# Moving one gather in 32 from GpSimd to SyncE and ScalarE in a two-layer graph kernel

## Chip, core and metric

The kernel runs on one core of one Trainium2 chip. The metric is the device time of one execution in microseconds; lower is better. The core has five engines with a queue each: TensorE (PE, with its weight loads shown as PEld), VectorE (DVE), ScalarE (ACT), GpSimd (POOL) and SyncE (SP), and 16 DMA engines that all queues share. In the rows below a name with a q (SPq, ACTq) is the queue of an engine: register work and the issue of transfers.

## What is computed

Two graph layers on 12500 nodes of 256 features and 200000 edges. The edges come sorted by dst. Each layer sums rows of a node table over the edges that end in a node, multiplies by weights, and normalizes.

```
# layer 0
out_deg = max(segment_sum(ones, src), 1)
t1  = x @ W1
msg = (t1[src] + (x[src] * x[dst]) @ W2) / (sqrt(out_deg[src]) * sqrt(out_deg[dst]))
embed = leaky_relu(where(in_cnt > 0, t1 + segment_sum(msg, dst), 0) + b)
x = layernorm(x + embed / max(norm(embed), 1e-12))
# layer 1
xt  = x @ W.T + b
out = segment_sum(xt[src], dst) / (deg + 1)
x = layernorm(x + out)
```

## The kernel before

The edges are cut into 1563 tiles of 128 edges, and 32 tiles make a round: 49 rounds per layer, the last with 27 tiles. One round also finishes one pair of node blocks (2 x 128 nodes).

GpSimd gathers. For each tile it issues one indirect DMA (L405) that reads 128 table rows of 1 KB, one for each edge, into one of 32 slots of `ring`. The indices stand in `idx`. TensorE multiplies each slot by a 0/1 matrix `dst_hot` (L1004), which adds the rows of a group of 8 tiles by destination into one of four sum buffers. After each of these it loads a register in `pace()` (L993). VectorE makes the 0/1 matrices (L710) and adds each group into `acc`, a view of `big` (L736).

ScalarE releases the slots. After each group k of round i has been multiplied (`groups_done`), `refill` copies the 8 indices of group k of round i+1 into `idx` (L514), and GpSimd waits for that copy only. So a gather of round i+1 may start once its group in round i has been multiplied.

Each round i also finishes the pair of blocks i-1. The steps stand in one fixed order on each engine:

- layer 0, VectorE: `mix` (L746, L748) after group 1. TensorE: transposes in `turn_halves` (L977) after tile 19, products with the weights (L988) after tile 23; these wait for `a_ready`.
- ScalarE, between the refills of groups 1 and 2: `clear_sums` (L521) in layer 0 or `take_sums` (L527) in layer 1, then `take_turned` (L536), two copies out of the banks into `a_t`, each of which sets `a_ready`. After the refill of group 2: `roots` (L542 and L544 in layer 0, L544 alone in layer 1). Then the refill of group 3.
- VectorE, after group 2: `finish_sums` and `moments`, with ScalarE's roots in between; after group 3: `norm`.
- SyncE, in `next_pair`: when `var_ready` comes, two loads of x (L304 in layer 0, L300 in layer 1), and when `out_ready` comes, two stores (L309, L313). It has nothing else to do in the rounds.

The order of work is written out by hand. Each engine runs its own queue in order, and only semaphores tie the engines together.

Of the kernel before, what the change touches and what calls it, by code (L numbers as in the profile page):

```python
# [24 lines left out]
P = 128  # L25
D = 256
KF = D // P
NODES = 12500
# [5 lines left out]
U = 32  # L34
# [35 lines left out]
DUMP = NPAD  # L70


def gnn(nc, x, src, dst, w1, w2, b0, wl, b1, out):
# [6 lines left out]
    with ExitStack() as ctx:  # L80
# [19 lines left out]
        src_hi = sb("src_hi", [P, TILES], BF16)  # L100
        count_to = sb("count_to", [P, P, PAIR], BF16)
# [115 lines left out]
        gather_turn = sem("gather_turn")  # L217
        dst_hot_made = sem("dst_hot_made")
# [42 lines left out]
        def _(sp):  # L261
# [69 lines left out]

            sp.wait_ge(flag_made, 1)
            disordered = sp.value_load(flag[0:1, 0:1], min_val=0, max_val=1)
            with sp.If(disordered == 0):
                for layer in range(2):
                    for s in range(2):
                        load_x(layer, 0, s, s)
                    with sp.Fori(0, ROUNDS - 2) as m:
                        next_pair(layer, m)
                    next_pair(layer, ROUNDS - 2)  # L340
# [28 lines left out]
        def _(g):  # L369
# [58 lines left out]
            with g.If(disordered == 0):  # L428
                for layer in range(2):
                    if layer == 1:  # L430
                        g.wait_ge(table1_whole, 1)
                    if layer == 1:
                        for q in range(4):
                            gather_quarter(layer, 0, q)
# [30 lines left out]
        def _(act):  # L465
# [80 lines left out]
            def round_(layer, i, finish):  # L546
                for q in range(4):
# [13 lines left out]
            with act.If(disordered == 0):  # L561
                for layer in range(2):
                    round_(layer, 0, False)
                    with act.Fori(1, ROUNDS) as i:
                        round_(layer, i, True)
# [333 lines left out]
        def _(pe):  # L899
# [95 lines left out]
            def round_(layer, i, finish, end=U):  # L995

                for k in range(GR):
# [3 lines left out]
                    for u in tiles:  # L1001
                        rounds_before = layer * (ROUNDS if u < FINAL else ROUNDS - 1) + i
                        pe.wait_ge(rows_in[u], 16 * (rounds_before + 1))
# [15 lines left out]
            with pe.If(disordered == 0):  # L1019
                for layer in range(2):  # L1020
                    round_(layer, 0, False)
                    with pe.Fori(1, ROUNDS - 1) as i:
                        round_(layer, i, True)
# [42 lines left out]
```

## Time and profile before

| what | value |
|---|---|
| median of 3 runs | 4180.89 us (4180.33 to 4181.39) |
| profiled execution | 4172.7 us, its span 4170.9 us |
| POOL busy | 3033.6 us, 73% |
| PE busy | 3387.3 us, 81% |
| DVE busy | 1603.1 us, 38% |
| ACT busy | 460.4 us, 11% |
| mean granted TensorE clock | 0.719 |
| DMA | 237098 packets, 489.88 MB, mean 117 GB/s |

Busy time leaves out the issue of transfers, register work and waits. A small share of busy time on ACT or SP therefore does not say how long its queue stands at a wait. The layers' rounds fill the span from about 240 to 4157 us; before them lies the preparation of the edges and of the scaled table, without gathers of the rounds.

### The profile page before, as it was taken

The page shows a single profiled execution, that of the slowest core. Times are in us where ns is not written, and L with a number is a line of the kernel's source. Part 1 is how long each engine was busy: PE and PEld are TensorE (multiplying, and loading weights), DVE is VectorE, ACT ScalarE, POOL GpSimd, SP SyncE. Part 2 cuts the span into 40 slices and gives each one's busy share as a digit, 9 for nine tenths or more (in the row PEclk, how much of TensorE's full clock was granted, in tenths as well). Part 3 has the DMA queues.
Part 4 walks back from the last instruction along what each step waited for, and adds up shares of the span by engine and source line. Part 5 has one row for each costly group of instructions (what it writes and reads, how often), then busy time and mean ns, then how long its engine had stood idle before and what let it go on. Part 6 is the DMA issues. An engine that isn't in the chain of part 4 may idle for free.

```text
span 4170.9 us, 49033 instructions
## 1 busy us (share of the span) xinstructions
PE 3387.3 (81%) x9623; PEld 1749.8 (42%) x9623; DVE 1603.1 (38%) x3315; ACT 460.4 (11%) x1457; POOL 3033.6 (73%) x3179
## 2 busy tenths in 40 slices
PE   6568888888888888888878887888888888888887
PEld 5434444444444444444443343334333343343433
DVE  9954334343343433434342323333233332333333
ACT  8910000000000000000000000000000000000000
POOL 5167777777777777777757777777777777777776
PEclk8777767777677776777776767767677667777666
DMA  6244444343443434444333444444443444434443
GB/s 189 68 138 119 114 120 119 114 119 114 119 119 114 119 114 120 119 115 120 115 94 111 119 115 119 114 120 117 118 119 114 120 117 117 120 114 119 117 117 106
DMA packets 237098, 489.88 MB, mean 117 GB/s; under 512 B 57665, under 2 KB 137044, under 8 KB 237076
## 3 DMA queue, kind: packets, MB, share of 16 engines
q0 software_dynamic: 151072, 409.95, 34.7%
q1 hardware_dynamic: 86004, 79.66, 5.9%
q8 instruction: 11, 0.18, 0.0%
q14 instruction: 11, 0.09, 0.0%
HBM read 450.84 MB, written 38.54 MB: 117 GB/s over the span
## 4 chain that ended last, share of the span: by engine, by line
POOL 68%; issue 25%; DVE 4%; PE 1%; DVEq 1%; POOLq 1%; DMA 0%; SPq 0%; ACT 0%; ACTq 0%
POOL ring L405 68%; DVE hot_space L600 2%; DVEq L592 0%; PE banks L1004 0%; DVE big L663 0%; PE banks L988 0%; POOLq L435 0%; POOLq L402 0%; PE banks L916 0%; DVE big L724 0%; POOLq L403 0%; DVEq L635 0%; DMA ring<-in_dst 0%; SPq L270 0%; DMA ring<-x,idx 0%
## 5 line engine op out<-in xcount | busy, mean ns | idle before, releaser
L1004 PE MATMUL banks<-ring,hot_space 128*128 128x257 f32 x6252 | 2901.9, 575 | 671.6 <-DMA ring<-x,idx 326.5
L1004 PEld LDWEIGHTS banks<-ring,hot_space 128*128 128x128 f32 x6252 | 1315.7, 256 | 2192.9 <-DMA ring<-x,idx 1045.3
L405 POOL DMA_INDIRECT ring<-x,idx x1563 | 1486.5, 951 | 505.7 <-issue 475.9
L405 POOL DMA_INDIRECT ring<-scaled_x,idx x1531 | 1455.9, 951 | 476.4 <-issue 465.6
L736 DVE SCALAR_TENSOR_TENSOR big<-banks,here_mask,big 128x257 f32 x784 | 343.7, 480 | 2086.7 <-PE banks L1004 2086.6
L710 DVE TENSOR_TENSOR hot_space<-banks,dst_rel 128x1024 f32<-128x1024 f32 x395 | 483.7, 1224 | 198.1 <-issue 197.6
L514 ACT COPY idx<-src_col 128x8 int32 (+1 forms) x392 | 77.3, 197 | 2528.2 <-PE banks L1004 2528.2
L988 PE MATMUL banks<-w_s,a_t 128*128 128x256 f32 x784 | 184.2, 389 | 0.0
L482 ACT ACTIVATE dst_rel<-columns,halves 128x128 bf16<-128x128 f32 x576 | 161.3, 374 | 4.5 <-DVE halves L629 4.5
L988 PEld LDWEIGHTS banks<-w_s,a_t 128*128 128x128 f32 x784 | 146.5, 192 | 34.6 <-issue 16.0
L977 PE MATMUL banks<-ident,halves 128*128 128x128 f32 x588 | 131.2, 388 | 13.2 <-DVE halves L748 8.7
L977 PEld LDWEIGHTS banks<-ident,halves 128*128 128x128 f32 x588 | 112.8, 207 | 46.6 <-issue 23.0
L916 PE MATMUL banks<-hot_space 128*128 128x98 bf16 x1280 | 91.1, 236 | 40.0 <-DVE hot_space L600 39.2
L536 ACT COPY a_t<-banks 128x512 f32<-128x512 f32 (+1 forms) x196 | 90.4, 479 | 282.6 <-PE banks L977 282.2
L413 POOL DMA_INDIRECT r_edge<-r_table,idx x32 | 32.0, 999 | 112.1 <-DMA r_table<-e 102.7
L988 PE MATMUL banks<-wt_s,a_t 128*128 128x256 f32 x392 | 106.1, 418 | 1.4
L916 PEld LDWEIGHTS banks<-hot_space 128*128 128x128 bf16 x1280 | 77.5, 113 | 51.7 <-DVE hot_space L600 44.8
L600 DVE TENSOR_TENSOR hot_space<-src_lo,count_to 128x2048 bf16<-128x2048 bf16 x80 | 97.6, 1221 | 0.2
L760 DVE SCALAR_TENSOR_TENSOR e<-banks,scal,b_s 128x256 f32<-128x256 f32 x98 | 42.9, 479 | 134.2 <-PE banks L988 134.2
L988 PEld LDWEIGHTS banks<-wt_s,a_t 128*128 128x128 f32 x392 | 76.8, 206 | 30.6 <-issue 20.2
L815 DVE TENSOR_SCALAR out_t<-out_t,mv,scal 128x256 f32<-128x256 f32 x196 | 75.7, 428 | 7.7
L600 DVE TENSOR_TENSOR hot_space<-src_hi,count_to 128x1568 bf16<-128x1568 bf16 x80 | 77.6, 969 | 0.0
(112 smaller groups left out, 773.5 us busy)
## 6 DMA issues: line engine op xcount, KB each, us to landing
ring<-x,idx POOLq DMA_INDIRECT x1563, 2.8
ring<-scaled_x,idx POOLq DMA_INDIRECT x1531, 2.8
x<-out_t SPq DMA_DIRECT2D x98, 128.0 KB, 2.6
x_t<-x SPq DMA_DIRECT2D x98, 128.0 KB, 2.3
big<-in_x SPq DMA_DIRECT2D x1, 12416.0 KB
x_t<-in_x SPq DMA_DIRECT2D x97, 128.0 KB, 2.2
result<-out_t SPq DMA_DIRECT2D x97, 128.0 KB, 1.9
scaled_x<-big SPq DMA_DIRECT2D x6, 1792.0 KB, 13.8
```

Of the source, the lines that this page charges most:

```text
L405: g.indirect_dma_start(ring[:, u, 0:D], None, table[layer], bass.IndirectOffsetOnAxis(ap=idx[:, u:u + 1], axis=0)).then_inc(rows_in[u], 16)
L482: last = nc.scalar.activation(steps[:, third, t, first:first + size], columns[:, 0:size], ACT.Sign, bias=step_digits[:, digit, bass.ds(n * ...
L514: nc.scalar.copy(idx[:, q * QT:(q + 1) * QT], src_col[:, bass.ds(i * U + U + q * QT, QT)]).then_inc(idx_ready, 1)
L536: nc.scalar.copy(a_t[s][:, 0:parts, :, :].rearrange("p h k n -> p (h k n)"), turned[s][:, 0:parts * D]).then_inc(a_ready[s], 1)
L600: last = nc.vector.tensor_tensor(hots[half], vals.unsqueeze(2).to_broadcast(shape), count_to[:, 0:size, :].unsqueeze(1).to_broadcast(shape ...
L710: last = nc.vector.tensor_tensor(dst_hot[:, buf, :, :], lane_row.unsqueeze(1).to_broadcast([P, GT, P]), rel, ALU.is_equal)
L736: last = nc.vector.scalar_tensor_tensor(here, group_sum(k), here_mask[:, n, bass.ds(i * GR + k, 1)], here, ALU.mult, ALU.add)
L815: nc.vector.tensor_scalar(out_t[s][:, :], out_t[s][:, :], mv[:, s, 0:1], scal[:, 6 + s:7 + s], ALU.subtract, ALU.mult).then_inc(out_ready[ ...
L916: last = nc.tensor.matmul(hist, lo_hot[half][:, t // PAIR, :, t % PAIR], hi_hot[half][:, t // PAIR, :, t % PAIR], start=first and t == 0, ...
L977: last = nc.tensor.transpose(turned[s][:, place:place + P], halves[:, s, h, k * P:(k + 1) * P], ident[:, :])
L988: last = nc.tensor.matmul(project[s], left, right, start=n == 0, stop=n == len(parts) - 1)
L1004: last = nc.tensor.matmul(group_sum(k), dst_hot[:, k % HOTS, u - k * GT, :], ring[:, u, 0:DW], start=u == tiles[0], stop=u == tiles[-1])
```

## The change

In rounds 2 to 47 of each layer (46 rounds, 23 pairs) GpSimd leaves out slot 31, the last of the round (`HAND_U`). For the even round of a pair SyncE fetches the 128 rows of that slot, for the odd round ScalarE. Each does it by 128 separate transfers of one row of 1 KB, whose address comes from a register. The indices are read with a DMA into one partition (`hand_idxs`) and from there into registers (`load`). The rows land in a buffer `hands`, and one more DMA copies the buffer into slot 31 of the ring. TensorE waits on that copy (`hand_in_ring`) in place of the gather. Both buffers lie in space that is free by then.

SyncE issues 64 rows after the copy into the ring and 64 after the next `next_pair`. ScalarE issues 26 rows after the refill of group 0, 12 after group 2's refill and the roots, and 26 after the refill of group 3, in every round of the pairs. GpSimd, ScalarE and TensorE now have loops over pairs or peeled rounds.

```diff
+HAND_U = U - 1
+HAND_REGS = 16
+ACT_ROWS = {0: (0, 26), 2: (26, 38), 3: (38, 64)}
+HAND_PAIRS = (ROUNDS - 2) // 2
...
 (SyncE)
+            def gather_by_hand(layer, j, half):
+                if half == 0:
+                    sp.wait_ge(hand_idx_in[0], 16 * (hand_no(layer, j) + 1))
+                    sp.sem_inc(sync_turn, 1)
+                for first in range(half * P // 2, (half + 1) * P // 2, HAND_REGS):
+                    sp.load(hand_regs, hand_idxs[0][0:1, first:first + HAND_REGS])
+                    for k in range(HAND_REGS):
+                        row = sp.snap(hand_regs[k], min_val=0, max_val=NODES - 1)
+                        sp.dma_start(hands[0][first + k:first + k + 1, :],
+                                     table[layer][bass.ds(row, 1), :]).then_inc(hand_rows_in[0], 16)
+            def hand_to_ring(layer, j):
+                sp.wait_ge(hand_rows_in[0], 16 * P * (hand_no(layer, j) + 1))
+                sp.wait_ge(groups_done, group_no(layer, 2 * j + 1, GR - 1) + 1)
+                sp.dma_start(ring[:, HAND_U, 0:D], hands[0][:, :]).then_inc(hand_in_ring[0], 16)
+            def hand_pair(layer, j):
+                next_pair(layer, 2 * j)
+                hand_to_ring(layer, j)
+                sp.wait_ge(hand_in_ring[0], 16 * (hand_no(layer, j) + 1))
+                gather_by_hand(layer, j + 1, 0)
+                next_pair(layer, 2 * j + 1)
+                gather_by_hand(layer, j + 1, 1)
+                load_hand_idx(layer, j + 2)
...
 (GpSimd)
-                    with g.Fori(1, ROUNDS - 1) as i:
+                    for i in range(0 if layer == 1 else 1, 2):
                         for q in range(4):
                             gather_quarter(layer, i, q)
+                    with g.Fori(2, ROUNDS - 1) as i:
+                        for q in range(4):
+                            gather_quarter(layer, i, q, HAND_U)
...
 (ScalarE)
+            def gather_by_act(layer, j, half, q):
+                if half == 0 and q == 0:
+                    act.wait_ge(hand_idx_in[1], 16 * (act_hand_no(layer, j) + 1))
+                    act.sem_inc(act_turn, 1)
+                    act.wait_ge(hand_in_ring[1], 16 * (act_hand_no(layer, j) + 1))
+                    act.sem_inc(act_turn, 1)
+                first, end = (half * P // 2 + n for n in ACT_ROWS[q])
+                act.load(act_regs[0:end - first], hand_idxs[1][0:1, first:end])
+                for k in range(first, end):
+                    row = act.snap(act_regs[k - first], min_val=0, max_val=NODES - 1)
+                    nc.scalar.dma_start(hands[1][k:k + 1, :],
+                                        table[layer][bass.ds(row, 1), :]).then_inc(hand_rows_in[1], 16)
+            def act_hand_to_ring(layer, j):
+                act.wait_ge(hand_rows_in[1], 16 * P * (act_hand_no(layer, j) + 1))
+                act.sem_inc(act_turn, 1)
+                nc.scalar.dma_start(ring[:, HAND_U, 0:D], hands[1][:, :]).then_inc(hand_in_ring[1], 16)
...
                     refill(layer, i, q)
                     if finish and q == LAST_K + 1:
                         roots(layer, i - 1)
+                    if pair_no is not None and q in ACT_ROWS:
+                        gather_by_act(layer, pair_no, half, q)
+                if pair_no is not None and half == 1:
+                    act_hand_to_ring(layer, pair_no)
...
 (TensorE)
+                        if u == HAND_U and by_hand is not None:
+                            pe.wait_ge(hand_in_ring[by_hand], 16 * (layer * HAND_PAIRS + pair_no + 1 + by_hand))
```

The first place is ScalarE in layer 0, at the refill of group 1 (rows L514 before, L579 after) and the copies into `a_t`. Before:

```order
L514 COPY idx<-src_col 128x8
L512 REGISTER_ALU
L514 ISA [waits groups_done]
L514 COPY idx<-src_col 128x8
L519 ISA
L521 ISA [waits mixed]
L521 COPY big<-zeros 128x514
L532 REGISTER_ALU
L536 COPY a_t<-banks 128x512 [waits halves_turned,projected]
```

After, from the last two rows of the burst behind group 0's refill on (L633 and L634 are one row's register work and its transfer):

```order
L633 ISA
L634 DMA src_lo<-scaled_x 1x256
L577 REGISTER_ALU
L579 ISA [waits groups_done]
L579 COPY idx<-src_col 128x8
L584 ISA
L586 ISA [waits mixed]
L586 COPY big<-zeros 128x514
L597 REGISTER_ALU
L601 COPY a_t<-banks 128x512 [waits halves_turned,projected]
```

The refill of group 1, the clearing and the copies into `a_t` now stand behind 26 transfers and one register load that were not there.

The second place is SyncE in layer 0, at the end of `next_pair`. Before:

```order
L309 ISA [waits out_ready0]
L309 DMA x<-out_t 128x256
L309 ISA [waits out_ready1]
L309 DMA x<-out_t 128x256
L338 REGISTER_ALU
L338 COMPARE_AND_BRANCH
```

After (L370 is the copy into the ring, L360 the load of 16 registers, L363 a row):

```order
L319 ISA [waits out_ready1]
L319 DMA x<-out_t 128x256
L368 ISA
L369 ISA [waits hand_rows_in0]
L370 DMA ring<-src_lo 128x256 [waits groups_done]
L376 REGISTER_ALU
L357 ISA [waits hand_in_ring0]
L360 TENSOR_LOAD src_hi [waits hand_idx_in0]
L362 ISA
L363 DMA src_lo<-scaled_x 1x256
```

Behind the stores SyncE now has waits for its rows, for the last group of the round and for the copy into the ring, and then 64 rows before the next pair's loads.

## Rows read from the trace of the kernel before

**Rows 1.** Page: the chain that ended last by engine, and TensorE's costliest group.
```profile
POOL 68%; issue 25%; DVE 4%; PE 1%; DVEq 1%; POOLq 1%; DMA 0%; SPq 0%; ACT 0%; ACTq 0%
...
L1004 PE MATMUL banks<-ring,hot_space 128*128 128x257 f32 x6252 | 2901.9, 575 | 671.6 <-DMA ring<-x,idx 326.5
```

**Rows 2.** Line L405, layer 0: ns min/median/max, first and last start.
```profile
L405 POOL DMA_INDIRECT ring<-scaled_x,idx x1531: 942/946/1227, 238.8 to 2159.7; - x192
```

**Rows 3.** Timeline of GpSimd in a round of layer 0: start, us, instruction.
```profile
1034.97 0.95 POOL L405 DMA_INDIRECT ring<-scaled_x,idx  x1 [0.30 <-issue]
```

**Rows 4.** Timeline of ScalarE, one round of layer 0.
```profile
1015.33 0.20 ACT L514 COPY idx<-src_col 128x8 int32 x1 [10.51 <-PE banks L1004]
...
1028.51 0.62 ACT L521 COPY big<-zeros 128x514 f32 x1 [3.02 <-DVE halves L748]
1030.99 0.58 ACT L536 COPY a_t<-banks 128x512 f32<-128x512 f32 x1 [1.86 <-PE banks L977]
...
1034.91 0.20 ACT L514 COPY idx<-src_col 128x8 int32 x1 [2.50 <-PE banks L1004]
...
1043.90 0.30 ACT L544 ACTIVATE scal<-mv,epsilon 128x2 f32<-128x2 f32 x1 [2.62 <-DVEq L592]
1044.92 0.20 ACT L514 COPY idx<-src_col 128x8 int32 x1 [0.72 <-PE banks L1004]
```

**Rows 5.** Timeline of TensorE, same round: the products.
```profile
1034.65 3.72 PE L988 MATMUL banks<-w_s,a_t 128*128 128x256 f32 x16
```

**Rows 6.** Timeline of ScalarE, one round of layer 1.
```profile
3018.14 0.62 ACT L527 COPY halves<-big 128x512 f32 x1 [0.87 <-DVE big L736]
3022.53 0.65 ACT L536 COPY a_t<-banks 128x256 f32<-128x256 f32 x2 [3.77 <-PE banks L977]
...
3031.66 0.29 ACT L544 ACTIVATE scal<-mv,epsilon 128x2 f32<-128x2 f32 x1 [4.93 <-DVEq L592]
```

**Rows 7.** Timeline with weight loads, same round: transposes and products.
```profile
3021.32 0.18 PEld L977 LDWEIGHTS banks<-ident,halves 128*128 128x128 f32 x1
...
3026.37 1.99 PE L988 MATMUL banks<-wt_s,a_t 128*128 128x256 f32 x8
```

**Rows 8.** Line L288, a transfer into one partition: ns min/median/max.
```profile
L288 SPq DMA_DIRECT2D base_row<-group_bases x1: 236/236/236, 183.3 to 183.3; - x1
```

**Rows 9.** DMA from 183.2 to 185.2 us, that transfer alone: packets, MB, share.
```profile
q1 hardware_dynamic: 2, 0.00, 0.1%
```

**Rows 10.** Line L304, transfers with an address from a register.
```profile
L304 SPq DMA_DIRECT2D x_t<-in_x x97: 342/355/1628, 220.6 to 2168.6; - x97
L304 SPq FUSED_REGOPS  x94: 55/65/81, 280.4 to 2128.9; - x94
L304 SPq MOVE x_t<-in_x x94: 29/29/29, 280.5 to 2129.0; - x94
```

**Rows 11.** Timeline of SyncE, one round of layer 0.
```profile
1003.83 0.91 SPq L304 DMA_DIRECT2D x_t<-in_x  x2
1006.75 0.91 SPq L309 DMA_DIRECT2D x<-out_t  x2
```

**Rows 12.** Line L993, a load of one register.
```profile
L993 PEldq TENSOR_LOAD <-block_row x3126: 296/302/758, 231.0 to 4155.0; - x196
```

**Rows 13.** Windows of 10 us: PE, PEld, DVE, ACT, POOL busy, PEclk, DMA share, GB/s.
```profile
1014.00:1024.00 10.00, 9.50 (x17) 4.03 (x17) 2.10 (x3) 0.20 (x1) 7.57 (x9) 0.50 0.36 105
...
1034.00:1044.00 10.00, 8.19 (x32) 5.67 (x32) 5.51 (x18) 0.49 (x3) 7.56 (x9) 1.00 0.36 105
```

**Rows 14.** Line L988, layer 0: ns min/median/max.
```profile
L988 PE MATMUL banks<-w_s,a_t x784: 378/379/797, 271.2 to 2180.4; 128*128 128x256 f32 x196
```

**Rows 15.** DMA from 1000 to 1080.4 us: queues, and the loads' landing.
```profile
q0 software_dynamic: 3072, 8.39, 36.3%
q1 hardware_dynamic: 1152, 1.05, 3.8%
...
x_t<-in_x SPq DMA_DIRECT2D x4, 128.0 KB, 2.1
```

More of the change, by code:

```diff
@@ L100, in gnn @@
         src_hi = sb("src_hi", [P, TILES], BF16)
+        hands = [src_lo[:, 2 * n * D:2 * (n + 1) * D].bitcast(F32) for n in range(2)]
+        hand_idxs = [src_hi[0:1, 2 * n * P:2 * (n + 1) * P].bitcast(I32) for n in range(2)]
         count_to = sb("count_to", [P, P, PAIR], BF16)
@@ L217, in gnn @@
         gather_turn = sem("gather_turn")
+        hand_idx_in = [sem(f"hand_idx_in{n}") for n in range(2)]
+        hand_rows_in = [sem(f"hand_rows_in{n}") for n in range(2)]
+        sync_turn = sem("sync_turn")
+        hand_in_ring = [sem(f"hand_in_ring{n}") for n in range(2)]
         dst_hot_made = sem("dst_hot_made")
@@ L334, in _ @@
             with sp.If(disordered == 0):
+                for c in range(len(X_CHUNKS)):
+                    sp.wait_ge(table_stored[c], 16)
                 for layer in range(2):
@@ L544, in roots, with act_hand_no, load_act_idx, round_ @@
                 nc.scalar.activation(pair[3], mv[:, :, 1], ACT.Sqrt, bias=epsilon[:, 0:1]).then_inc(var_rooted, 1)
-            def round_(layer, i, finish):
+            act_regs = [act.alloc_register(f"act_row{k}") for k in range(26)]
+            def act_hand_no(layer, j):
+                return layer * HAND_PAIRS + j
+            def load_act_idx(layer, j):
+                nc.scalar.dma_start(hand_idxs[1][:, :],
+                                    src[bass.ds((2 * j + 3) * U * P + HAND_U * P, P)].rearrange("(a n) -> a n", a=1)
+                                    ).then_inc(hand_idx_in[1], 16)
+            def gather_by_act(layer, j, half, q):
[14 more added lines that the diff above has]
+                nc.scalar.dma_start(ring[:, HAND_U, 0:D], hands[1][:, :]).then_inc(hand_in_ring[1], 16)
+            def round_(layer, i, finish, pair_no=None, half=0):
+                if pair_no is not None and half == 0:
+                    load_act_idx(layer, pair_no)
                 for q in range(4):
@@ L561, in _ @@
             with act.If(disordered == 0):
+                act.sem_inc(hand_in_ring[1], 16)
+                for c in range(len(X_CHUNKS)):
+                    act.wait_ge(table_stored[c], 16)
                 for layer in range(2):
+                    if layer == 1:
+                        act.wait_ge(table1_whole, 1)
                     round_(layer, 0, False)
-                    with act.Fori(1, ROUNDS) as i:
-                        round_(layer, i, True)
+                    with act.Fori(0, HAND_PAIRS) as j:
+                        round_(layer, 2 * j + 1, True, j, 0)
+                        round_(layer, 2 * j + 2, True, j, 1)
+                    round_(layer, ROUNDS - 2, True)
+                    round_(layer, ROUNDS - 1, True)
                     if layer == 0:
@@ L993, in pace, with round_ @@
                 pe.value_load(block_row[0:1, 0:1], min_val=0, max_val=NW - 1)
-            def round_(layer, i, finish, end=U):
+            def round_(layer, i, finish, end=U, by_hand=None, pair_no=0):
                 for k in range(GR):
@@ L1021, in _ @@
                     round_(layer, 0, False)
-                    with pe.Fori(1, ROUNDS - 1) as i:
-                        round_(layer, i, True)
+                    round_(layer, 1, True)
+                    with pe.Fori(0, HAND_PAIRS) as j:
+                        round_(layer, 2 * j + 2, True, by_hand=0, pair_no=j)
+                        round_(layer, 2 * j + 3, True, by_hand=1, pair_no=j)
                     round_(layer, ROUNDS - 1, True, FINAL)
```

34 lines of the change are left out of this document (27 added, 7 removed).

## The prediction

> **What bounds the kernel now.** I read the chain of waits first. It should show GpSimd with the issue gaps between its instructions holding nearly all of the span, and TensorE with idle time that a DMA ended [rows 1]: the gathers set the pace and TensorE waits for them. Next the timeline of GpSimd: a gather of 0.95 us follows the last after 0.30 us of issue, so one costs 1.25 us and no semaphore stands between [rows 3]. From the first and last start of layer 0, 1920.9 us over 1530 steps is 1.2555 us, and 32 of them make a round of 40.18 us [rows 2]. Last I read ScalarE's timeline, because the new work goes there. It looks idle, but three of its stops in a round are waits in a fixed order: on a group, on the transposes before the copies into a_t, and on VectorE for the roots [rows 4, 6].
>
> **What goes.** GpSimd leaves out one gather in 46 rounds of each layer, 92 in all. 92 x 1.25 = 115.0 us [rows 3], and the round becomes 38.93 us if GpSimd still sets it. The profiled execution is 4172.7 us, so that alone gives 4057.7; the median of the runs stands 8.2 above it, which makes 4065.9. What comes next behind GpSimd decides the rest.
>
> **What one row costs the queue that issues it.** No transfer of one row from a register address is in the trace. A transfer into one partition holds SyncE's queue for 0.236 us [rows 8]. Two transfers with register addresses take 0.91 us from the start of one to the end of the other, and each is 0.355, so 0.20 us lies between them: the fused register work of 0.065, a move of 0.029 and gaps [rows 10, 11]. A row thus costs 0.236 + 0.20 = 0.436 us, and I take that on both queues. The low bound is 0.29, the issue and about 0.05 of gap, if the register work is hidden. The high bound is 0.555, the whole step of a 128-row transfer. A register load is 0.30 [rows 12] and with its gap 0.35; I take this for each load of 12 to 26 registers. The far bound is 0.30 for every register, 64 x 0.30 = 19 us a round; I stay with the one instruction, since it is one.
>
> **SyncE.** For a pair of rounds it has 128 x 0.436 = 55.8, eight loads 2.8, eight large transfers in four steps of 0.91, 3.6, its ring copy 0.36 with about 2.1 of landing [rows 10, 15], and some 0.5 for the indices and the branch: 65.2. It also stands 2.0 us twice between the loads of x and the stores [rows 11]: 69 of 77.9 us. It fits, with 9 us left. Behind its waits stand the loads of x for the next mix and the stores, and both have more than ten microseconds until VectorE asks. I cost SyncE at nothing; it would set the pace from a row of 0.50 us on.
>
> **ScalarE.** Here I add up the circle that its queue must close in each round, if it comes late and TensorE waits for it.
> Layer 0, from the first copy into a_t: the copy 0.58, about 0.15 to TensorE, then from the start of the products at 1034.65 to the end of the second root at 1044.20, 9.55 [rows 4, 5]. That is 10.3 us in which ScalarE can issue no row, because the roots stand ahead of the 12 rows. Then the three remaining refills, 0.20 of copy and 0.1 of register work each, 0.9; three register loads, 1.05; the clearing of the sums 0.62 with gaps, 0.8; at the pair's end the landing of the last row 2.1, the copy's issue 0.36 and the next index load about 0.3, per round 1.4. Sum 14.4 us without rows. The 64 rows are 27.9. Together 42.3 us, against 38.93 for the gathers and 40.18 now.
> Layer 1, from take_sums: 0.62, 0.1, the transposes until the copies start 1.2 (3021.32 to 3022.53), one copy 0.33, 0.15, and from the start of the products at 3026.37 to the end of the root at 3031.95, 5.6 [rows 6, 7]: 8.0. With 0.9, 1.05, 1.4 and 0.1 it is 11.4, with the rows 39.3 us.
> In between the two sits a smaller term. The products ran where the granted clock was 1.00 (2.4 GHz), just after TensorE had worked through its stretch at 0.50 (1.2 GHz) [rows 13]. A TensorE that is kept waiting for a_t may run them at the lower level, where one matmul takes 797 ns and not 379 [rows 14]. For the whole set that is at most 3.7 us in layer 0 and 2.0 in layer 1 (their own length again); the least is nothing. I take a fifth, 0.7 and 0.4.
> The rounds then are 43.0 and 39.7 us.
>
> **The sum.** 46 x (43.0 - 40.18) = +130, 46 x (39.7 - 40.18) = -22, together +108 us: 4280.7 in the profiled execution's terms, with the 8.2 us 4289. The 115 us that GpSimd gives back are not to be added; they are the difference to a bound that then no longer holds. The tail, the fetch of the first rows in each layer and the waits for the table (stored long before) I cost at nothing: the first hand slot is wanted at the end of round 2, some 110 us after the layer begins, and 128 rows take 56.
> TensorE itself is no term. Its 671.6 us of waits on DMA [rows 1] are 6.9 us a round, and it gives 1.25 of them away. A late ring copy has a round's slack.
>
> **The rivals.**
> The first is that rows are cheap. In terms of the row price c, layer 0 needs 14.4 + 64c and layer 1 11.4 + 64c. Both fit under 38.93 from c = 0.38 down, and then the whole 115 us come: 4066. With the clock term the kernel is even with before at about c = 0.41. At c = 0.29 ScalarE has 6 us to spare. For it: two register operations might overlap the transfer before; the distance to my 0.436 is small. Against it: on SyncE they visibly did not overlap [rows 11].
> The second is that the two queues hinder each other when both issue. SyncE issues in 56 of some 84 us; if one's 0.236 us had to wait for the other's, a row would grow by 0.03 to 0.05 on average, and to 0.47 where they alternate. At 0.47, layer 0 is 45.2 and layer 1 41.9 with the clock term: 46 x (5.0 + 1.7) = +308, or 4489. If every row cost 0.555, it would be 50.6 and 47.3, +807 or 4988, with SyncE the bound as well (128 x 0.555 + 13.4 = 84.4 per pair). Nothing in the trace speaks to it, since ScalarE issues no transfer in it.
> The Trainium skill, in Perfetto Trace Analysis, section DMA Instruction — HWDGE (DVE, Sync), says that such transfers use one descriptor generator that two sequencers share, and that it is locked for exclusive use. By that rule this rival would hold and the time be near 4489; no run so far shows it.
> The third is that all rows go through one DMA engine. The transfer into one partition left two packets, one of data and one to signal, so it ran on a single engine [rows 9]. All 16 engines were busy 40.1% [rows 15], 31 us of a pair. The hardware queue's mean packet cost is 3.8% x 16 x 80.4 / 1152 = 42 ns; 256 rows with two packets each add 22 us if they all meet on one engine: 53 of 78 us, which is no bound. It decides only from 0.18 us a row on. If a row had to land (about 2.1 us [rows 15]) before that queue's next row moved, a pair would take 128 x 2.1 = 269 us, and the kernel over 12,000.
> On this the Trainium skill, in DMA: Bandwidth & Descriptors, section Why a DMA increments its semaphore by 16 and not by 1, says that a transfer that uses fewer than 16 engines takes the lowest-numbered ones. By that rule all 256 rows of a pair do meet on the first engine; the two packets above agree with one engine, and which one they do not show.
>
> **How the numbers follow.** ScalarE's circle sets the round, with c between 0.41 and 0.46: 0.44, time 4289, its own range 4190 to 4440. Rows cheap enough for a gain: 0.30, times 4066 to 4172. The queues hinder each other: 0.18, 4440 to 4990. One engine or a SyncE bound far above: 0.04. A result within 0.2% of before, which is about what a measurement can tell from no change, is the narrow passage between the first two: 0.04. So faster 0.30, same 0.04, slower 0.66. The range runs from 4062, the whole gain, to 4520, which leaves out the harder half of the second rival and the one engine.
>
> **What would show it.** In the changed profile the steps between rows on ScalarE should be about 0.44 us. The copies into a_t should come right behind the burst and the refill of group 1, TensorE should wait for them before the products in layer 0, and the refills of groups 0 and 1 should come late after their groups. A round should take about 43 us in layer 0 and under 40.2 in layer 1; the layers should differ. GpSimd should then wait for the refill in each round of layer 0, where it now waits for nothing. SyncE should reach its wait for var_ready before it comes. I am wrong if ScalarE still stands waiting for groups 0 and 1 in both layers: then the rounds are 38.9 us and the gain is whole. Steps above 0.5 us, or longer issues where both queues are at work, speak for the second rival; gathers that land much later than before for the third.

## The result, and the profile after

The changed kernel takes 5175.7 us, the median of 4 runs (5172.2 to 5176.3), against 4180.9 for four runs of the kernel before beside it (4180.3 to 4181.4). The ratio is 1.238, 95% interval 1.236 to 1.240: slower, as forecast, but by 995 us and not by 108, and outside the range of 4062 to 4520. The experiments ran in four groups, each on a chip of its own beside the kernel before: in two groups that took about 4171 us, in two 5031 to 5040, and there the two queues' register steps, 44 ns otherwise, took up to 1.5 us (the disturbed chips below). Ratios are taken only within a group.

The page after: the chain that ended last by engine and by line, then three of the costliest groups, with what they waited for in the last column.

```profile
ACTq 53%; issue 18%; PE 10%; DVE 8%; DVEq 4%; DMA 3%; ACT 3%; POOL 2%; SPq 0%; POOLq 0%
ACTq L634 29%; ACTq L631 18%; PE banks L1099 6%; ACTq L633 5%; PE banks L1120 4%; DVEq L703 3%; DVE hot_space L711 2%; POOL ring L470 2%; DMA src_hi<-in_src 1%; PE banks L1088 1%; DVE stats L914 1%; ACT idx L579 1%; DMA src_lo<-x 1%; DMA src_lo<-scaled_x 1%; ACT halves L592 1%
...
L470 POOL DMA_INDIRECT ring<-scaled_x,idx x1485 | 1420.9, 957 | 1074.4 <-ACT idx L579 636.7
...
L1099 PE MATMUL banks<-w_s,a_t 128*128 128x256 f32 x784 | 291.6, 552 | 1245.9 <-ACT a_t L601 1245.9
L1088 PE MATMUL banks<-ident,halves 128*128 128x128 f32 x588 | 120.4, 342 | 1256.1 <-ACT halves L592 1221.7
```

GpSimd held 68% of the chain before [rows 1] and holds 2% now; ScalarE's queue holds 53%: 29% in the issue of its rows (L634) and 18% in its register loads (L631). TensorE, which had waited for a DMA, now waits some 27 us in each of the 46 rounds for a copy that ScalarE makes: `a_t` (L601) in layer 0, `halves` (L592) in layer 1. GpSimd waits for the refills. That is the mechanism that the forecast named, ScalarE's circle, at another size.

ScalarE's timeline over one pair of rounds of layer 0, which answers to [rows 4]: start, length, instruction, count in a burst, and in brackets the idle time before. The stretch from 1506.67 to 1612.52 is one pair.

```profile
1506.67 0.20 ACT L579 COPY idx<-src_col 128x8 int32 x1 [7.54 <-issue]
1512.55 10.16 ACTq L634 DMA_DIRECT2D src_lo<-scaled_x  x26
1523.90 0.50 ACTq L641 DMA_DIRECT2D ring<-src_lo  x1
1527.43 0.23 ACTq L619 DMA_DIRECT2D src_hi<-in_src  x1
...
1531.37 10.20 ACTq L634 DMA_DIRECT2D src_lo<-scaled_x  x26
1541.84 0.20 ACT L579 COPY idx<-src_col 128x8 int32 x1 [13.68 <-issue]
...
1542.63 1.07 ACT L601 COPY a_t<-banks 128x512 f32<-128x512 f32 x2
...
1554.37 0.29 ACT L609 ACTIVATE scal<-mv,epsilon 128x2 f32<-128x2 f32 x1 [2.62 <-DVEq L703]
1557.31 4.65 ACTq L634 DMA_DIRECT2D src_lo<-scaled_x  x12
1562.22 0.20 ACT L579 COPY idx<-src_col 128x8 int32 x1 [7.56 <-PE banks L1120]
1568.10 10.16 ACTq L634 DMA_DIRECT2D src_lo<-scaled_x  x26
...
1612.52 0.20 ACT L579 COPY idx<-src_col 128x8 int32 x1 [7.52 <-issue]
```

The copies into `a_t` stand right behind a burst and a refill, as expected. What was not expected is the time between a refill and the burst that follows it: 5.9 us ahead of the bursts at 1512.55 and 1568.10, 3.4 ahead of 1531.37. Behind the last root it is 2.9, ahead of 1557.31. In it the queue loads index registers. Line L631, ScalarE's register loads, in three short stretches (at 1506.7: 26 words from word 102 of the tile, 38 into its second half; at 1529.1: 26 words from word 0; at 1554.4: 12 words from word 26), and for the whole run, then a row's own instructions and SyncE's loads of 16 words (ns min/median/max, first and last start):

```profile
L631 ACTq TENSOR_LOAD <-src_hi x1: 5702/5702/5702, 1506.7 to 1506.7; - x1
L631 ACTq TENSOR_LOAD <-src_hi x1: 2129/2129/2129, 1529.1 to 1529.1; - x1
L631 ACTq TENSOR_LOAD <-src_hi x1: 2767/2767/2767, 1554.4 to 1554.4; - x1
...
L631 ACTq TENSOR_LOAD <-src_hi x276: 2107/2780/6327, 258.6 to 5103.5; - x138
L634 ACTq DMA_DIRECT2D src_lo<-scaled_x x2944: 213/214/531, 261.0 to 2686.6; - x197
L633 ACTq FUSED_REGOPS  x5888: 44/44/56, 260.8 to 5118.9; - x197
L363 SPq DMA_DIRECT2D src_lo<-scaled_x x2944: 224/225/332, 231.6 to 2593.7; - x197
L360 SPq TENSOR_LOAD <-src_hi x368: 1137/1232/1631, 230.2 to 5023.4; - x184
```

A row is 0.39 us on ScalarE (10.16 / 26): issue 214 ns, a fused register step of 44, a move of 29, and gaps. Two loads of 26 words each differ by 3.6 us. Their places in the round and their first words differ; the experiments tell which of the two it is.

SyncE in the same stretch:

```profile
1504.58 31.18 SPq L363 DMA_DIRECT2D src_lo<-scaled_x  x64
1535.99 0.23 SPq L350 DMA_DIRECT2D src_hi<-in_src  x1
1554.54 0.94 SPq L314 DMA_DIRECT2D x_t<-in_x  x2
...
1558.60 0.52 SPq L370 DMA_DIRECT2D ring<-src_lo  x1
1563.52 31.21 SPq L363 DMA_DIRECT2D src_lo<-scaled_x  x64
```

From 1536.0 to 1563.5 it issues hardly anything, and ScalarE's rows are no faster there: 4.65 / 12 = 0.39, as in the bursts at 1512.55 and 1568.10 under which SyncE is busy throughout. Last, TensorE's clock and the same products, which answer to [rows 13] and [rows 5]: windows with PE, PEld, DVE, ACT and POOL busy, granted clock, DMA share and GB/s; then the timeline.

```profile
1530.00:1540.00 10.00, 0.00 (x0) 0.00 (x0) 0.00 (x0) 0.00 (x0) 6.64 (x7) 0.50 0.39 110
1540.00:1550.00 10.00, 6.74 (x23) 5.67 (x24) 1.05 (x3) 1.89 (x5) 5.63 (x6) 0.65 0.23 66
1550.00:1560.00 10.00, 9.77 (x39) 6.50 (x37) 7.70 (x22) 0.50 (x2) 7.56 (x9) 1.00 0.50 147
```

```profile
1543.26 5.57 PE L1099 MATMUL banks<-w_s,a_t 128*128 128x256 f32 x16 [30.92 <-ACT a_t L601]
```

TensorE stood still for ten microseconds and more, the clock was granted at 0.50 (1.2 GHz), and the products began at that level: 5.57 us, against 3.72 before.

### The profile page after: what moved, and what is told of

Read it like the earlier page. It is cut to its first block, busy times and chain, and to the rows that moved or that the text cites. A ratio compares the mean times of both kernels' runs of the same rounds, so it can differ in the third digit from the quotient of the medians.

```text
span 5174.5 us, 85381 instructions
## 1 busy us (share of the span) xinstructions
PE 2447.7 (47%) x9623; PEld 1620.5 (31%) x9623; DVE 1584.0 (31%) x3315; ACT 448.9 (9%) x1457; POOL 2952.9 (57%) x3087
## 3 DMA queue, kind: packets, MB, share of 16 engines
q14 instruction: 521, 4.27, 0.3%
## 4 chain that ended last, share of the span: by engine, by line
ACTq 53%; issue 18%; PE 10%; DVE 8%; DVEq 4%; DMA 3%; ACT 3%; POOL 2%; SPq 0%; POOLq 0%
ACTq L634 29%; ACTq L631 18%; PE banks L1099 6%; ACTq L633 5%; PE banks L1120 4%; DVEq L703 3%; DVE hot_space L711 2%; POOL ring L470 2%; DMA src_hi<-in_src 1%; PE banks L1088 1%; DVE stats L914 1%; ACT idx L579 1%; DMA src_lo<-x 1%; DMA src_lo<-scaled_x 1%; ACT halves L592 1%
## 5 line engine op out<-in xcount | busy, mean ns | idle before, releaser
L470 POOL DMA_INDIRECT ring<-scaled_x,idx x1485 | 1420.9, 957 | 1074.4 <-ACT idx L579 636.7
L470 POOL DMA_INDIRECT ring<-x,idx x1517 | 1441.1, 950 | 991.1 <-ACT idx L579 524.6
L1120 PE MATMUL banks<-ring,hot_space 128*128 128x257 f32 x6252 | 1852.5, 426 | 126.7 <-issue 43.4
L1120 PEld LDWEIGHTS banks<-ring,hot_space 128*128 128x128 f32 x6252 | 1131.6, 202 | 797.8 <-issue 554.1
L1099 PE MATMUL banks<-w_s,a_t 128*128 128x256 f32 x784 | 291.6, 552 | 1245.9 <-ACT a_t L601 1245.9
L1088 PE MATMUL banks<-ident,halves 128*128 128x128 f32 x588 | 120.4, 342 | 1256.1 <-ACT halves L592 1221.7
L1099 PEld LDWEIGHTS banks<-w_s,a_t 128*128 128x128 f32 x784 | 223.2, 292 | 1314.2 <-ACT a_t L601 1265.2
L1088 PEld LDWEIGHTS banks<-ident,halves 128*128 128x128 f32 x588 | 78.8, 169 | 1306.2 <-ACT halves L592 1241.3
L579 ACT COPY idx<-src_col 128x8 int32 (+1 forms) x392 | 77.6, 198 | 3830.3 <-issue 3376.7
L1099 PEld LDWEIGHTS banks<-wt_s,a_t 128*128 128x128 f32 x392 | 89.9, 230 | 19.0 <-ACT a_t L601 0.5
L601 ACT COPY a_t<-banks 128x512 f32<-128x512 f32 (+1 forms) x196 | 88.5, 478 | 61.2 <-PE banks L1088 54.9
L914 DVE BATCH_NORM_STATS2 stats<-out_t 128x6 f32<-128x256 f32 x196 | 73.8, 418 | 7.2
```

What stands on the lines that cost most here:

```text
L470: g.indirect_dma_start(ring[:, u, 0:D], None, table[layer], bass.IndirectOffsetOnAxis(ap=idx[:, u:u + 1], axis=0)).then_inc(rows_in[u], 16)
L1088: last = nc.tensor.transpose(turned[s][:, place:place + P], halves[:, s, h, k * P:(k + 1) * P], ident[:, :])
L1099: last = nc.tensor.matmul(project[s], left, right, start=n == 0, stop=n == len(parts) - 1)
L1120: last = nc.tensor.matmul(group_sum(k), dst_hot[:, k % HOTS, u - k * GT, :], ring[:, u, 0:DW], start=u == tiles[0], stop=u == tiles[-1])
```

## Experiments

The theory after the result was: ScalarE's circle is the bound and its rows cost what was forecast; the excess is in the register loads. Rivals: the two queues slow each other, the copy's landing at the pair's end, or TensorE's clock.

**Loads removed.** Three runs of the same kernel; it gathers the rows of the first 26 indices over and over, so the indices of the other rows are left out. s1 is the run to read, the other two met the chip of 5031 to 5040 us.

```diff
-                act.load(act_regs[0:end - first], hand_idxs[1][0:1, first:end])
...
+                    act.load(act_regs[0:26], hand_idxs[1][0:1, 0:26])
                     with act.Fori(0, HAND_PAIRS) as j:
```

> ScalarE loads its 26 registers once per layer and not three times a round; everything else, the 64 rows and their register work too, stays. It leaves out fetching the right rows for ScalarE's slot. Theory (ScalarE's circle sets the round and its three register loads, 2.1 + 2.8 + 5.7 = 10.5 us a round, are the term that the prediction had at 1.05): rounds fall from 52.9 and 50.2 us to about 42.4 and 39.7, the time to 5176 - 92 x 10.5 = about 4210 us. Rival 1 (the time that the trace shows as loads is a wait for transfers or code, which then falls on the rows): the steps between rows grow, and the time stays above 4900. Rival 2 (another engine is close behind): the rounds stop falling at some 45 us, about 4600.

> ScalarE loads its 26 registers once per layer and not three times a round; the 64 rows and their register work stay. It leaves out fetching the right rows for ScalarE's slot. Theory (ScalarE's circle sets the round and its three register loads, 2.1 + 2.8 + 5.7 = 10.5 us a round, are the term that the prediction had at 1.05): rounds fall from 52.9 and 50.2 us to about 42.4 and 39.7, the time by 92 x 10.5 = 966 us, a ratio to the kernel before of about 1.007. Rival 1 (the time shown as loads is a wait for transfers or code, which then falls on the rows): steps between rows grow, ratio above 1.17. Rival 2 (another engine stands close behind): rounds stop falling at some 45 us, ratio about 1.09.

> The same kernel as the first: ScalarE loads its 26 registers once per layer and not three times a round; its rows and their register work stay, and it leaves out fetching the right rows for its slot. The earlier executions stood on a chip where single register steps of SyncE's and ScalarE's queues took up to 1.4 us and the kernel before took 5031 us. Theory (ScalarE's circle without the 10.5 us of loads): on a chip where the kernel before takes about 4181 us, 4210 us, rounds of 42.4 and 39.7. Rival (the time of the loads falls on the rows): above 4900. Rival (SyncE stands close behind, with 77 us of work for a pair): rounds of up to 43 in both layers, about 4450.

e1 took 6378.8 us beside 5030.8; r1 6495.4, ratio 1.289 (1.285 to 1.293): slower than the changed kernel's 1.238 elsewhere. In both the long register steps sit in the rows themselves, and SyncE's queue holds 56% and 53% of the chain, so these two say nothing of ScalarE's loads. The trace of e1, SyncE's register steps:

```profile
L362 SPq FUSED_REGOPS  x5888: 2/44/1413, 231.7 to 6273.3; - x197
```

s1: 4194.3 us (4192.4 to 4196.1) beside 4170.3, ratio 1.0057 (1.0037 to 1.0077), where 1.007 was expected. All but 24 of the 995 us are gone with one instruction taken away. Its timeline, layer 0:

```profile
1542.02 0.20 ACT L579 COPY idx<-src_col 128x8 int32 x1 [4.50 <-issue]
1542.17 9.92 ACTq L633 DMA_DIRECT2D src_lo<-scaled_x  x26
...
1592.33 0.51 ACTq L640 DMA_DIRECT2D ring<-src_lo  x1
...
1676.71 0.51 ACTq L640 DMA_DIRECT2D ring<-src_lo  x1
```

Rows now follow the refill at once. The pair between the two ring copies takes 84.4 us; the average of layer 0 is 83.5 (22 pairs from the copy at 337.11 to the one at 2174.50), 41.8 per round, where 42.4 was expected. In layer 1 a pair takes 79.8 on average, 39.9 per round, expected 39.7.

**The price of a load, by itself.** The kernel before with 22 loads at the end of each of the two queues. In e4 nothing read the registers, the loads were dropped when the program was built, and the run (5035.3 beside 5030.8) says nothing of the price. r4 lets a one-row transfer use each.

```diff
+                sp.load(tried[0:12], words[0:1, 26:38])
+                sp.dma_start(src_lo[7:8, 0:512].bitcast(F32),
+                    table[1][bass.ds(sp.snap(tried[11], min_val=0, max_val=NODES - 1), 1), :]).then_inc(sp_tried, 16)
```

> The kernel before, with 22 register loads at the very end of SyncE's and of ScalarE's queue, of 1 to 26 registers from places 0 to 38 words into a row that starts on a round address; nothing uses them. It measures the price of a load by itself. Theory (price by count and start): from place 0 about 0.3 us + 0.06 to 0.08 a register, 12 registers 1.0 to 1.2 and 26 registers 2.1; 12 from place 26 2.8 us and 26 from place 38 5.7 us, on both queues. Rival (only ScalarE's loads are slow, or only beside traffic): all loads of one count cost the same whatever the place. The time of the kernel rises by some 50 us at its end, which says nothing.

> The kernel before, with 22 register loads at the very end of SyncE's and of ScalarE's queue, of 1 to 26 registers from places 0 to 38 words into a row of indices, each load followed by one row transfer that uses its last register. It measures the price of a load by itself. Theory (price by count and start): from place 0 about 0.3 us + 0.06 to 0.08 a register, 12 registers 1.0 to 1.2 and 26 registers 2.1; 12 from place 26 2.8 us and 26 from place 38 5.7 us, on both queues. Rival (only ScalarE's loads are slow, or only beside other work): all loads of one count cost the same whatever the place.

r4 took 5111.8 us beside 5039.8, on a disturbed chip; it is one run, with each load once on either queue. Four of SyncE's loads, in this order: 12 words from word 0, 26 from 0, 12 from 26, 26 from 38.

```profile
L359 SPq TENSOR_LOAD <-src_hi x1: 974/974/974, 5063.2 to 5063.2; - x1
L363 SPq TENSOR_LOAD <-src_hi x1: 2080/2080/2080, 5066.3 to 5066.3; - x1
L365 SPq TENSOR_LOAD <-src_hi x1: 2699/2699/2699, 5068.8 to 5068.8; - x1
L367 SPq TENSOR_LOAD <-src_hi x1: 5499/5499/5499, 5072.0 to 5072.0; - x1
```

The others, SyncE | ScalarE in ns: 1 word 446 | 458, 2 words 697 | 692, 4 words 532 | 632, 8 words 759 | 751, 16 words 1200 | 1217; 12 words from words 4, 8, 16 or 32 between 977 and 988, from word 1 or 2 between 2697 and 2808; from 26, 4 words 1099 | 1112, 8 words 1897 | 1955, 16 words 3500 | 3634, but 16 from 8 1209 | 1227. So a load that starts on a multiple of four words (16 bytes) costs about 0.3 us and 0.22 for each four words; from any other place tried (1, 2, 26, 38) it costs about 0.3 us and 0.2 for each single word. 26 words from 0 are six fours and two singles: 0.3 + 6 x 0.22 + 2 x 0.22 = 2.1. The two queues agree within 5% from 8 words on, and the kernel's own trace agrees too: 2.13, 2.77 and 5.70. Nothing else ran beside these loads, so the price does not come from the round.

**Only the places changed.** e2 copies the indices to places 0, 32 and 48 of each half and keeps the split 26, 12, 26; e7 keeps the copy and splits 24, 16, 24.

```diff
+ACT_PLACE = {0: 0, 2: 32, 3: 48}                       (e2)
-ACT_ROWS = {0: (0, 26), 2: (26, 38), 3: (38, 64)}
+ACT_ROWS = {0: (0, 24), 2: (24, 40), 3: (40, 64)}      (e7)
```

> ScalarE's indices are laid out so that each of its three loads starts on a multiple of 64 bytes (places 0, 32 and 48 of each half); counts 26, 12, 26 stay; the index transfer becomes three small ones. Theory (a load's price goes by where it starts: 0.08 us a register on a round address, as for SyncE and the first burst, 0.22 elsewhere): the second load falls from 2.8 to about 1.2 us, the third from 5.7 to 2.1, so 5.1 us a round less and 0.25 us more for the two transfers: 5176 - 92 x 4.9 = about 4725 us. Rival (the third load is slow because of what stands before it in the round: the copy of the indices, or traffic of the other queue): loads stay at 2.8 and 5.7 us, the time within 5100 to 5200.

> The changed kernel with one line different: ScalarE's bursts are 24, 16 and 24 rows, so that each load starts on a multiple of four registers' words (16 bytes). Theory (a load costs 0.3 us and 0.22 for each group of four words on such a place, or for each single word elsewhere): the loads cost 1.65 + 1.2 + 1.65 = 4.5 us a round and not 10.5; 92 x 6.0 = 552 us less than 5176: 4624 us, ratio to before 1.106, rounds of 46.9 and 44.2. Rival (the load's price comes from what runs beside it): rounds above 50, ratio above 1.2.

e2 took 6449.2 us beside 5030.8 on a disturbed chip; its time can't be used, but its loads can. e7: 4641.2 us (4638.4 to 4644.0) beside 4171.9, ratio 1.1125 (1.1103 to 1.1148), expected 1.106. The loads of both:

```profile
L635 ACTq TENSOR_LOAD <-src_hi x276: 961/2115/2815, 298.2 to 6362.6; - x138
```

```profile
L631 ACTq TENSOR_LOAD <-src_hi x276: 1179/1660/2060, 259.3 to 4576.5; - x138
```

The median of e2's loads is that of 26 words from a good place, and the 5.7 us are gone. In e7 three loads of a round cost 1.66 + 1.2 + 1.66 = 4.5 and not 10.5, 6.0 less; the pair went on average from 105.8 to 94.5 us in layer 0 and from 100.7 to 88.8 in layer 1, 5.7 and 6.0 per round. Over 46 rounds each that is 535 us, and the kernel took 534 us less than the changed one (on another chip, where the kernel before took 9 us less).

**One queue alone.** In e3 and r3 (the same kernel) ScalarE gathers its tile and SyncE nothing; in r5 and s5 the other way round. GpSimd gathers the tile that is given back, so it leaves out one slot in 64.

```diff
                     with g.Fori(0, HAND_PAIRS) as j:
                         for q in range(4):
-                            gather_quarter(layer, i, q, HAND_U)
+                            gather_quarter(layer, 2 * j + 2, q, HAND_U)
+                        for q in range(4):
+                            gather_quarter(layer, 2 * j + 3, q, U)         (s5; e3 has them the other way)
```

> SyncE fetches no rows; GpSimd gathers slot 31 of the even rounds again and leaves it out in the odd ones only; ScalarE as in the changed kernel. Theory (ScalarE's circle alone sets the round, the two queues do not hinder each other): step between ScalarE's rows stays 0.39 us, the time 5150 to 5190 us although half of the moved gathers are back. Rival (the queues hinder each other): ScalarE's step falls to 0.35 us or less, 64 x 0.04 x 92 = 235 us less, about 4940.

> SyncE fetches no rows; GpSimd gathers slot 31 of the even rounds again and leaves it out in the odd ones only; ScalarE as in the changed kernel. Theory (ScalarE's circle alone sets the round, the two queues do not hinder each other): the step between ScalarE's rows stays 0.39 us, the ratio to before stays 1.23 to 1.24 although half of the moved gathers are back. Rival (the queues hinder each other): ScalarE's step falls to 0.35 us or less, 64 x 0.04 x 92 = 235 us less, ratio about 1.18.

> SyncE fetches slot 31 of the even rounds as in the changed kernel; ScalarE fetches no rows and has its old loop; GpSimd gathers slot 31 of the odd rounds again. Theory (only ScalarE's circle cost time): GpSimd sets the round again, 46 gathers less, 46 x 1.25 = 57.5 us, ratio to before 0.986. Rival (SyncE is a bound too: two bursts of 31.2 us, four steps of 0.9, its landing and waits come to some 77 us against 79.1 for a pair): its waits for var_ready vanish and the pair takes over 80 us, ratio 1.00 to 1.03.

> Again: SyncE fetches slot 31 of the even rounds, ScalarE fetches nothing, GpSimd gathers slot 31 of the odd rounds. Theory (only ScalarE's circle cost time): 46 gathers less, 57.5 us, 4123 us where before takes 4181. Rival (SyncE's 77 us of work for a pair, with its waits, do not fit in 79.1): 4181 to 4300, and its waits for var_ready are gone.

e3 took 6174.6 beside 5030.8; r3 6222.9, ratio 1.235 (1.231 to 1.239); r5 7016.2, ratio 1.393 (1.386 to 1.399), all on the disturbed chips, where in r5 SyncE's queue held 55% of the chain (its register step went up to 1.4 us, as in e1). They tell nothing of the undisturbed case; ScalarE alone was not run on an undisturbed chip. s5: 4115.4 us (4114.3 to 4117.5) beside 4170.3, ratio 0.9868 (0.9851 to 0.9884), where 0.986 was expected: it beats both kernels. Its chain, and one of SyncE's bursts:

```profile
POOL 69%; issue 24%; DVE 3%; PE 1%; DVEq 1%; POOLq 1%; DMA 0%; ACT 0%; SPq 0%; ACTq 0%
```

```profile
1512.69 31.32 SPq L363 DMA_DIRECT2D src_lo<-scaled_x  x64
```

GpSimd is the bound again, and the gain is what it leaves out: 46 x 1.25 = 57.5 us forecast by the price of a gather, 54.9 measured. SyncE's bursts last as long without ScalarE's rows as with them (31.3 and 31.2 us): at this density the queues do not hinder each other. How close SyncE came to being the bound, its waits for var_ready show (in us: total, times, longest):

```profile
SPq L314 <- DVEq L702: 110.9, 6, 36.4
SPq L310 <- DVEq L702: 108.5, 4, 34.3
```

Only three of these ten waits, 3.7 us together, fall in the pairs of layer 0 and none in those of layer 1; the others stand where a layer ends or begins.

**Rows ahead of the roots.** e8 is e7 with each burst of the third quarter moved into the time in which VectorE works toward the roots.

```diff
                     refill(layer, i, q)
-                    if finish and q == LAST_K + 1:
-                        roots(layer, i - 1)
                     if pair_no is not None and q in ACT_ROWS:
                         gather_by_act(layer, pair_no, half, q)
+                    if finish and q == LAST_K + 1:
+                        roots(layer, i - 1)
```

> As e7_aligned, and the 16 rows behind the refill of group 2 stand ahead of the roots and not behind them. Theory (ScalarE's circle holds about 7.7 us in layer 0 and 4.9 in layer 1 in which it waits for VectorE with nothing to issue; a burst of 1.2 + 16 x 0.39 = 7.4 us fits there wholly in layer 0 and delays the root by 2.5 us in layer 1): rounds of 39.5 and 39.3 us, 46 x (78.8 - 80.4) = 72 us less than before, 4109 us where before takes 4181, ratio 0.983. Rival 1 (the roots come late enough to delay VectorE, the store and the next copy): rounds of 42 or more, ratio above 1.04. Rival 2 (SyncE, with 77 us of work a pair, now stands at the bound): rounds of 40, ratio 1.00.

e8: 4150.9 us (4148.1 to 4154.2) beside 4171.9, ratio 0.9951 (0.9934 to 0.9967), expected 0.983. Faster, clear of the interval, by less than a third of what was expected:

```profile
ACTq 46%; issue 21%; PE 13%; DVE 6%; DMA 5%; ACT 3%; POOL 3%; DVEq 3%; SPq 0%; POOLq 0%
```

```profile
1513.98 0.20 ACT L579 COPY idx<-src_col 128x8 int32 x1 [11.14 <-issue]
...
1516.46 6.17 ACTq L634 DMA_DIRECT2D src_lo<-scaled_x  x16
1523.25 0.20 ACT L607 ACTIVATE scal<-scal 128x2 f32<-128x2 f32 x1 [7.32 <-DVEq L703]
...
1557.03 0.20 ACT L579 COPY idx<-src_col 128x8 int32 x1 [12.25 <-issue]
...
1592.85 0.20 ACT L579 COPY idx<-src_col 128x8 int32 x1 [11.06 <-issue]
```

The burst now hides in the wait, but ScalarE still sets the pace: the round that holds the pair's end takes 43.1 us (1513.98 to 1557.03), the other 35.8, together 78.9 here. The two rounds are not levelled, and the long one is far above 38.9. From ring copy to ring copy the pairs take 80.4 us on average in layer 0 and 80.9 in layer 1, where the kernel before takes 80.4 and the theory wanted 78.8: once settled, e8 is no faster than the kernel before. Its 21 us come from the start of each layer, where GpSimd has a lead: by the starts of its gathers the first 14 of the hand rounds (the 46 with a slot fetched by hand) in layer 0 and 12 in layer 1 take 39 us each, and then the rounds lengthen to ScalarE's pace. The rounds of 40 are what the second rival had named, but no part of the chain lies on SyncE's queue (SPq 0%).

## Why the forecast was right in kind and wrong in size

**The bound moved to ScalarE's circle: right.** The chain, TensorE's waits for `a_t` and `halves`, and GpSimd's waits for the refill show it, and the layers differ: 105.9 us for this pair (1506.67 to 1612.52) in layer 0, 105.8 on average, and 100.7 in layer 1, where four pairs lie between the two ring copies below. But layer 1 was to stay under 40.2 a round and takes 50.35.

```profile
3811.76 0.50 ACTq L641 DMA_DIRECT2D ring<-src_lo  x1
...
4214.57 0.50 ACTq L641 DMA_DIRECT2D ring<-src_lo  x1
```

**The step that failed** is the sentence on register loads: 0.30 us for one register and with its gap 0.35, "I take this for each load of 12 to 26 registers". Three loads measured 2.13 + 2.77 + 5.70 = 10.6 us a round, not 1.05, on the path in both layers: 9.55 x 92 = 879 us, where the time missed the forecast by 887. The experiments show it: s1, without the loads, comes to a ratio of 1.0057, and e7, with loads 6.0 us a round cheaper, to 1.1125. That 879 comes so near 887 is partly luck. A round missed by 9.9 us in layer 0 and by 10.65 in layer 1, whose terms are not taken apart here; over 46 rounds that is 945 us, 66 more than the loads, and the lead of GpSimd below takes 49 off. The last 9 are how far the profiled executions stand from the medians, 8.2 below before and 0.6 above after. The row the step rested on [rows 12] showed the load of one register, and nothing bounded 26 of them but the guess that was set aside, 19 us a round. With the ends at 1.05 and 19 us a round, the range should have taken in the middle. The Trainium skill, in Runtime: NRT & Kernel Launch, section Instruction fetch mechanics, states about 200 ns per register even for bulk, of another kind of load. The runs agree for a load from a place off a multiple of four words (0.20 to 0.22 each) and differ for the rest, a quarter of that. By that figure, as an estimate, 64 words would have been 12.8 us a round, near the 10.6.

**The other terms**, for a round of layer 0, forecast and measured:

| term | forecast | measured | from |
|---|---|---|---|
| 64 rows | 27.9 | 25.0 | 64 x 0.39 |
| first copy into `a_t` to the last root, with the clock | 11.0 | 12.0 | 1542.63 to 1554.66 |
| three register loads | 1.05 | 10.6 | above |
| the pair's end, per round | 1.4 | 3.1 | 1522.71 to 1529.1, less a refill, halved |
| refills and clearing | 1.7 | about 2.2 | remainder, not measured by itself |
| sum | 43.0 | 52.9 | 105.85 / 2 |

Without the loads these terms miss by -2.9, +1.0, +1.7 and +0.5 us, together +0.3: the sum beside the loads came out right because a dear row price hid three terms that were too small. s1 says the same: with 1.05 us a round put back for the loads, as forecast, its +24 us would be about +121 (an estimate, 24 + 92 x 1.05), against the +108 of the forecast.

Rows were 0.39 and not 0.436 on ScalarE: the register step is 44 ns there and not 65, the issue 214 and not 236. On SyncE, 31.2 us less three loads of 1.23 are 0.43 a row, as forecast. The clock took 1.85 us of the products where 0.7 was set; the cause is the one named, TensorE kept waiting, and the wait became much longer. At the pair's end 2.7 us lie between the ring copy's end and the next loads of indices (1524.40 to 1527.43 less the register work), where the loop jumps back; on this below.

**The sum.** Rounds of 52.9 and 50.35 give 46 x (52.9 + 50.35 - 80.36) = +1053, and the median rose 995. The rest is what GpSimd keeps of its lead. From the first to the last gather of a layer, less 23 pairs, the kernel before has 73 and 113 us [rows 2], the changed one 2484.0 - 23 x 105.8 = 51 and 2401.6 - 23 x 100.7 = 86: 49 us less, which closes the sum to 1004 (the spans of the two profiles differ by 1003.6). The starts of the gathers show where it is: GpSimd enters the hand rounds ahead of ScalarE, and the first two of them take 38.9 and 47.2 us in layer 0 and 38.9 each in layer 1, before they settle at ScalarE's pace. s1 agrees: 46 x (41.8 + 39.9 - 80.36) = +62, less 40 by the same count, and +24 measured. This term was missing in the forecast.

GpSimd's gathers in the changed kernel, for the two spans used here (as [rows 2] for layer 0 before; its layer 1 went from 2190.5 to 4151.9):

```profile
L470 POOL DMA_INDIRECT ring<-x,idx x1517: 942/949/1146, 2753.1 to 5154.7; - x190
L470 POOL DMA_INDIRECT ring<-scaled_x,idx x1485: 942/949/1194, 238.5 to 2722.5; - x186
```

**GpSimd's saving: right.** 92 gathers went, and since another bound held, nothing came of it. Where GpSimd stays the bound nearly the full price comes back, as in s5 (54.9 of 57.5 us).

**SyncE at nothing: right, but not with 9 us left.** In the changed kernel it waits for var_ready for 1192 us in all (638.0 and 554.2), since ScalarE's circle is so long. In s5 it starts layer 0 late, and as it catches up, with no wait for var_ready before 600 us, a pair from ring copy to ring copy takes it 76.6 to 77.9 us, where the forecast had 69. Most of the difference is again the loads: eight of them are 8 x 1.23 = 9.9 us and not 2.8. So in s5, at 79.1 us for a pair of GpSimd's rounds, 1 to 3 us a pair are left, and at the 77.9 that the whole gain wanted SyncE would have stood at the bound itself.

**The rivals.** Cheap rows: c came to 0.39, just above the 0.38 where the whole gain was to come, and the gain did not come, since the circle held 9.55 us that this rival too had left out. Queues that hinder each other: the trace speaks against a cost at this density, and so against the time of 4489 that the forecast drew from the lock on the descriptor generator in the Trainium skill, Perfetto Trace Analysis, section DMA Instruction — HWDGE (DVE, Sync): ScalarE's rows take 0.39 with SyncE busy and silent, SyncE's bursts 31.2 and 31.3. At closer spacing it was not tried. One engine: the gathers land 2.8 us after their issue, before and after, and rows issue every 0.39 us without waiting for one another, so it is out as a bound; whether all rows meet on one engine, as the forecast took from the Trainium skill, DMA: Bandwidth & Descriptors, section Why a DMA increments its semaphore by 16 and not by 1, was not seen.

## What to carry to other kernels

A register load is not a single cheap instruction: price it by its number of registers and its first word, keep the first word on a multiple of four, and make no forecast from the row of a one-register load. When work is given to an engine that looks idle, add up what it must finish between two of its fixed waits, at the real price of each piece; if the sum comes near the round, give the work to the engine whose waits have slack, here SyncE alone, 1.3% faster and then nearly full. Work put inside a wait does hide there (e8), but that alone did not bring the round below the old one. A kernel whose engine has a lead at the start hides a slower pace for a while, so read the pace from rounds in the middle.

## What the runs showed of the hardware that was not expected

- A load of registers from the on-chip memory (r4): about 0.3 us and 0.22 per four words from a multiple of four words, 0.3 us and 0.2 to 0.21 per single word from the other places tried. 26 words are 2.1 us or 5.5 to 5.7.
- ScalarE's pair loop leaves a gap of some 2.7 us where it jumps back. The queue of instruction fetches moved 521 packets and 4.27 MB, where the kernel before had 11 and 0.09. The row of the page after (packets, MB, share):

```profile
q14 instruction: 521, 4.27, 0.3%
```

  The Trainium skill, in Runtime: NRT & Kernel Launch, section Instruction fetch mechanics, says that a taken branch to a place outside the held window must fetch it first. The gap and the packets agree with that, and one such packet is moved between 1523.9 and 1527.5 us, around the gap. SyncE's pair loop shows a gap of the same size in s5 (1544.47 to 1547.34). No run took the jump away, so the cause is not shown.
- A one-row transfer with its address from a register costs its queue 0.39 us on ScalarE and 0.43 on SyncE (after), with the other queue busy or silent.
- On the two disturbed chips these queues' register steps took up to 1.5 us instead of 0.044, and the same kernel that is 1.3% faster elsewhere (s5) was 39% slower (r5), with SyncE's queue at 55% of the chain. The kernel before, with few such steps, took 21% longer there than elsewhere (5035 against 4171); what ails these chips no run shows.
